# Light hops of a fused graph network: the edge-weight multiply moves from VectorE to GpSimd

## The reference

```python
def _L1_gnn_ref(ebds, edge_val, edge_row, edge_col, num_layers):
    def spmm(x):
        msgs = edge_val[:, None] * x[edge_col]
        return jax.ops.segment_sum(msgs, edge_row, num_segments=n)
    acc = ebds
    cur = ebds
    for _ in range(num_layers):
        cur = spmm(cur)
        acc = acc + cur
    return acc
...
h = jnp.maximum(_layernorm(x, axis=-1), 0.0)
x = x + _L1_gnn_ref(h, edge_weight, src, dst, 3)
```

## Time and profile before

| | |
|---|---|
| three runs | 6606.59, 6608.01, 6619.2 us |
| median | 6608.01 us |
| profiled execution | 6613.96 us, its span 6612.3 us |
| busy share of the span | DVE 64%, POOL 57%, PE 52%, ACT 44% |
| the phase touched | POOL's first gather at 2852.66 us, DVE's last chain of the third hop at 4061.5 us |
| length of the phase between its barriers | about 1,230 of 6,612 us |

### The profile page before, as it was taken

One profiled execution on the slowest core, in us unless ns is written; L12 is line 12 of the kernel. 1 busy time (PEld: TensorE's weight loads), 2 busy tenths in 40 slices (PEclk: granted clock), 3 DMA queues, 4 the chain that ended last, 5 costly groups with the idle time before them and its releaser, 6 DMA issues. The chain is left out here.

```text
span 6612.3 us, 76481 instructions
## 1 busy us (share of the span) xinstructions
PE 3439.3 (52%) x17336; PEld 2399.6 (36%) x17522; DVE 4231.7 (64%) x15945; ACT 2904.3 (44%) x7008; POOL 3787.8 (57%) x3751
## 2 busy tenths in 40 slices
PE   1527776501620000047777775888879994444443
PEld 0414555401620000024444443566546663433222
DVE  7369996361571646679999997777646664544332
ACT  1936775200300001146776764777647663322110
POOL 1655563676666734565353544666477635776777
PEclk9769997755865555568998987999989996656666
DMA  2225665408612264433344443555434435755333
GB/s 65 79 74 178 201 199 174 138 12 145 198 39 47 37 163 152 140 110 108 98 114 102 107 108 117 183 188 190 138 101 137 134 115 195 225 178 173 115 120 103
DMA packets 509434, 859.79 MB, mean 130 GB/s; under 512 B 109352, under 2 KB 169108, under 8 KB 507885
## 3 DMA queue, kind: packets, MB, share of 16 engines
q1 hardware_dynamic: 393227, 662.54, 31.4%
q0 software_dynamic: 115808, 192.94, 12.9%
HBM read 412.62 MB, written 454.37 MB: 131 GB/s over the span
## 5 line engine op out<-in xcount | busy, mean ns | idle before, releaser
L2936 POOL DMA_INDIRECT gcn_ring<-GT,gcn_index x588 | 586.2, 997 | 199.4 <-issue 171.0
L1578 POOL DMA_INDIRECT light_ring<-C,light_s_u x392 | 393.7, 1004 | 313.7 <-DVE light_acc L1621 206.3
L3037 DVE SCALAR_TENSOR_TENSOR gcn_acc<-gcn_acc,cont,gcn_ring 128x128 f32<-128x128 f32 x588 | 203.8, 347 | 565.7 <-DMA gcn_ring<-GT,gcn_index 564.5
L3119 PE MATMUL gcn_psA<-ident,gcn_h 128*128 128x128 f32 x588 | 153.6, 412 | 611.8 <-DVE gcn_h L3040 611.3
L3086 ACT ACTIVATE gcn_hT<-gcn_psA 128x512 f32<-128x512 f32 x147 | 87.9, 598 | 705.6 <-PE gcn_psA L3119 705.4
L3119 PEld LDWEIGHTS gcn_psA<-ident,gcn_h 128*128 128x128 f32 x588 | 99.3, 206 | 649.2 <-DVE gcn_h L3040 649.2
L1421 ACT ACTIVATE tail_h<-tail_x,tail_nmr,tail_std 128x128 f32<-128x128 f32 x784 | 320.6, 483 | 10.0 <-DVE tail_nmr L1352 10.0
L2190 POOL DMA_INDIRECT out<-source_x,source_own_u x196 | 194.3, 991 | 210.5 <-DVE source_x L2276 162.4
L1777 PE MATMUL so_ps<-ordered,shift 128*128 128x1 f32 x2 | 0.6, 363 | 560.2 <-DVE so_diag L1760 560.2
L476 POOL DMA_INDIRECT gat_rows<-T,src_u x196 | 186.2, 950 | 184.2 <-POOLq L1108 75.1
L476 POOL DMA_INDIRECT got_s<-TAB,src_u x196 | 197.6, 1008 | 163.9 <-DMA got_s<-TAB,src_u 66.7
(11 more groups left out here) (589 smaller groups left out, 13493.9 us busy)
## 6 DMA issues: line engine op xcount, KB each, us to landing
T<-front_t SPq DMA_DIRECT2D x196, 272.0 KB, 2.1
C<-light_acc SPq DMA_DIRECT2D x147, 256.0 KB
source_c<-C SPq DMA_DIRECT2D x147, 256.0 KB
GT<-source_r SPq DMA_DIRECT2D x147, 256.0 KB, 2.1
gcn_own<-GT SPq DMA_DIRECT2D x147, 256.0 KB
RC<-gcn_own SPq DMA_DIRECT2D x147, 256.0 KB
gat_rows_r<-RG SPq DMA_DIRECT2D x104, 264.0 KB
RG<-gat_rows SPq DMA_DIRECT2D x2, 12936.0 KB
```

Source lines behind the costliest of these rows:

```text
L1578: nc.gpsimd.indirect_dma_start(out=ring[:, n % RING, j, :], out_offset=None, in_=tables[h], in_offset=bass.IndirectOffsetOnAxis(ap=index[: ...
L2936: nc.gpsimd.indirect_dma_start(out=ring[:, n % RING, j, :], out_offset=None, in_=net.GT[i], in_offset=bass.IndirectOffsetOnAxis(ap=index[: ...
L3037: nc.vector.scalar_tensor_tensor(out=acc[:, n % 2, j, :], in0=before, scalar=net.cont[:, c:c + 1], in1=ring[:, n % RING, j, :], op0=ALU.mu ...
L3119: ins = nc.tensor.transpose(psA[n % 2][:, j * P:(j + 1) * P], h[:, n % 2, j, :], net.ident[:, :])
```

## The change

The multiply by the edge weights leaves DVE's queue and goes to POOL's. POOL does it three groups behind its gathers (BEHIND = 3): after the four gathers of group g it waits for the rows of group g-3 and multiplies them in place; after the last gathers of a hop it multiplies the last three. DVE keeps the wait on `weighed` and the chain.

```diff
--- before.py
+++ after.py
@@ -1543,7 +1543,7 @@
 
 
     s_ = net.S
-    RING, AR = 8, 6
+    RING, AR, BEHIND = 8, 6, 3
     total = HOPS * NG
     sums_of = lambda n: range(0) if n % HOP_STEPS >= SUM_STEPS or n // HOP_STEPS >= HOPS else range(
         n // HOP_STEPS * NG + n % HOP_STEPS * NG // SUM_STEPS, n // HOP_STEPS * NG + (n % HOP_STEPS + 1) * NG // SUM_STEPS)
@@ -1567,6 +1567,11 @@
                 nc.gpsimd.tensor_copy(s_u[:, :], s_.s[:, :]).then_inc(copied, 1)
                 nc.gpsimd.tensor_copy(at[:, :], s_.first_end[:, :]).then_inc(copied, 1)
                 pool.wait_ge(copied, 3)
+
+                def weigh(n):
+                    g, got = n % NG, ring[:, n % RING, :, :]
+                    pool.wait_ge(arrived[n % RING], 16 * S * (n // RING + 1))
+                    nc.gpsimd.tensor_tensor(got, got, s_.ew[:, g * S:(g + 1) * S].unsqueeze(2).to_broadcast([P, S, D]), ALU.mult).then_inc(weighed, 1)
                 for h in range(HOPS):
                     index = s_u if h else r_u
                     for g in range(NG):
@@ -1578,6 +1583,10 @@
                             nc.gpsimd.indirect_dma_start(
                                 out=ring[:, n % RING, j, :], out_offset=None, in_=tables[h],
                                 in_offset=bass.IndirectOffsetOnAxis(ap=index[:, c:c + 1], axis=0)).then_inc(arrived[n % RING], 16)
+                        if g >= BEHIND:
+                            weigh(n - BEHIND)
+                    for n in range((h + 1) * NG - BEHIND, (h + 1) * NG):
+                        weigh(n)
                     for k in range(AR):
                         pool.wait_ge(stored[k], 16 * len(range(k, (h + 1) * NG, AR)))
                     nc.gpsimd.indirect_dma_start(out=fix[h][:, :], out_offset=None, in_=tables[h + 1],
@@ -1607,9 +1616,6 @@
 
                 def sums(n):
                     g = n % NG
-                    got = ring[:, n % RING, :, :]
-                    v.wait_ge(arrived[n % RING], 16 * S * (n // RING + 1))
-                    nc.vector.tensor_tensor(got, got, s_.ew[:, g * S:(g + 1) * S].unsqueeze(2).to_broadcast([P, S, D]), ALU.mult).then_inc(weighed, 1)
                     v.wait_ge(weighed, n + 1)
                     v.wait_ge(cleared, 1)
                     if n >= AR:
```

## The result

| | before | changed |
|---|---|---|
| median, us | 6612.18 (4 runs) | 6683.44 (4 runs, 6680.51 to 6689.92) |
| ratio to before | | 1.0109, 95% 1.0091 to 1.0126 |
| profiled execution, us | 6613.96 | 6680.51, span 6678.8 |

The changed kernel is slower by 71 us; the forecast was +66, from 6608 to 6674.

A forecast was written before the change was run, and what follows sets the result against it. DVE was taken to bound two-group steps, ACT's string one-group steps. Removal -66, unhidden holds +111, start +18 and other hop starts and ends +3 gave +66 on 6608: 6674 us, range for 8 in 10 6603 to 6728.

The forecast's parts named there:

- the removal: Taking the multiply off DVE saves 1.38 us in each of 48 two-group steps, nothing in one-group steps: -66 us.
- the start: At the beginning of a hop, more gathers and POOL's multiplies precede DVE's first chains, shifting the whole pipeline: +18 us.
- first chain, group 3: DVE's first chain comes 14.3 us later, and the multiply of group 3 ends 17.7 us later than its chain started.
- The holds: DVE instructions with two SBUF inputs stand still during POOL's two-input multiply; 111 us not hidden, made of 45 + 66.
- the mean over phases: Hold cost averaged over all positions in DVE's step: 0.88 us a hold, +0.8 us a period, +39 us in all.
- the walk: One three-group period followed in order: holds hit beta, late chain and x3; 25.25 us against 24.15, +54 us in all.
- The floor: ACT's string x0T, h, yn sets 6.51 us from late place to gamma, so no step is shorter than 11.28 us.
- The length of the hold: POOL's multiply blocks DVE from 0.62 us before its recorded start to 0.13 before its end: 1.58 us.
- Rival B: The hold is no longer than POOL's instruction, 0.43 us each on average: 6616 us, no change that can be told; chance 0.18.
- Rival C: DVE is first nearly every time and POOL waits, so no holds and a faster kernel: 6563 us; chance 0.12.
- Rival D: POOL, its multiply stretched by DVE, becomes the bound: 6629 us at least, near 6700 with the holds; chance 0.20 with them.
- the starts of hops two and three: POOL starts two steps before DVE needs the first group; counted as 1 us for each of these hops.

The follow-up runs named there:

- the idle multiply: Changed kernel, but POOL multiplies into a scratch buffer nobody reads and DVE sums unweighted rows without waiting for it; disturbed runs, ratios to before 0.9927 and 0.992.
- the write-only fill: Like the idle multiply, but POOL fills a 128x1152 scratch tile with zeros, reading nothing; disturbed runs, ratios to before 0.9825 and 0.9835.
- the timed multiply: Changed kernel, with POOL's one or two multiplies per step held until DVE's x3 add is done; undisturbed 6553.35 against 6593.04 us before, ratio 0.9936.

## Why the prediction was right

By its own steps, with what the runs gave; the kernel with no multiply stands between before and changed, so its phase splits the loss.

| step | predicted | measured |
|---|---|---|
| the removal | -66 | 1149.7 - 1208.9 = -59 (ratio 0.9907: -61) |
| two steps without multiplies | 22.77 | 22.93 |
| holds and start, against no multiply | 111 + 18 + 3 = 132 | 1283.3 - 1149.7 = 134 |
| the start, first g2T against before | +18 | 82.0 - 62.7 = +19.3 |
| first chain, group 3 | +14.3, +17.7 | +13.5, +15.8 |
| two steps changed | 25.25 | 25.45 |
| POOL's multiply | 1.09 | 1.05 |
| sum | +66 | +71 (phase +74) |

**The holds** were the deciding term, and the forecast had them right in kind (the idle multiply has them, the write-only fill and the timed multiply don't) and in place (beta, late chain, x3). The excess of chain, beta, x3 and gamma is 146 us, 0.99 a multiply, where the mean over phases gave 0.88. Of it, 134 less the start's 23.9 (first g2T 82.0 against 58.1) = 110 us isn't hidden; predicted 111. That this agrees to 1 us is luck: the 111 was made of a net 45 and a removal of 66, and behind the first g2T the runs give a net 74.4 - 19.3 = 55 and a removal of 55. The two misses, of 10 and 11 us, cancel in the 111; in the sum the net stayed 10 us too small. Between the walk (+54) and the mean (+39) I took +45; the walk, which followed actual positions, was the better of the two, and its 1.1 us for two steps is the measured difference of the means (24.80 - 23.66 = 1.14). Its three places are those of the middle of a hop only.

**The floor** is shown by the kernel with no multiply: gamma's idle time for yn is 72.7 us there, 28.2 before. The term, 66, was too large. Behind the first g2T the removal gave back 1146.2 - 1091.6 = 55 us, and another 4.6 came at the start (first g2T 58.1 against 62.7), where none was counted. The step that was off is "11.49, still above the floor": the floor of 6.51 us from late place to gamma was read from one row, but ACT's yn comes at 7.20 us or later in steps where DVE alone needs 6.7, so 18 of 43 two-group steps run into it, and give back 1.20 us in the mean instead of 1.38. What moves is the start of x0T, which waits for PE's psF (2.1 to 3.1 us behind the late place in the steps of 6.19 and 7.20 us); from x0T to gamma it is 4.07 us. Why psF comes at different times was not looked into.

**The length of the hold.** 0.62 + 1.09 - 0.13 = 1.58 was drawn from two rows, and it holds in many: of the 57 instructions in which a multiply starts, the one that was furthest on had started 0.61 us ahead of POOL; in the kernel whose product nobody uses, 72 of 74 were held, and the two that weren't had started 0.66 and 0.67 us ahead. Beta's first row in the period above starts 0.37 us before POOL's multiply and loses 1.3, and the x3 row starts 0.48 us after POOL's recorded start and loses only 0.44: 3173.25 + 0.44 = 3173.69, 0.13 us before POOL's end at 3173.82. So the end of the hold, 0.13 us before POOL's recorded end, came out again. Beta's own work began at 3158.24 + 1.31 = 3159.55, 0.12 before the end at 3159.67. The prediction's sentence on these rows says too much, though: with an add of 1.28 us its hold of 0.62 + 1.28 - 0.13 = 1.77 us is 0.5 us longer than the instruction and not 0.6, and if the one that issues first were the one that keeps going, the trace doesn't agree, since by the recorded starts DVE was first there (4112.54 against 4113.16), as in all 57. Whether POOL issues earlier than its record says is open. Rival B, a hold that is no longer than the instruction, had foretold half the loss; it falls with the 0.99 us a multiply. Rival C (DVE first, POOL waits) falls with beta's 1263 ns. Rival D falls with the 140.8 us for which POOL still waits for DVE; its multiply isn't stretched either, 1051 ns in the mean.

**Counted, but not met**: the tiny nmr instructions stood among those that are held, after the 1.77 us row. They can be: in the timed kernel their maximum is 1594 ns. In the changed kernel it is 203 ns, since POOL's multiplies never fell on them. And the starts of hops two and three cost nothing: 20.9 us from first gather to first chain, 20.6 before.

## What to carry to other kernels

Before arithmetic goes to an idle GpSimd, ask what VectorE does at that moment, not only how much room GpSimd has: here an instruction of 1.05 us with two SBUF inputs took 0.99 us from VectorE's two-input instructions beside it, more than the 0.66 us it relieved VectorE of. The same move with the same instructions gains once a semaphore puts it beside VectorE's PSUM and one-input stretch (ratio 0.9936 against 1.0111). And find the floor first, over many steps and not in one row: of 101 us removed from the busiest engine, only some 60 came back, the rest turned into a wait for the next engine.

## What the runs showed that was not expected

- A GpSimd fill of 128x1152 (1.08 us), as frequent as the multiply, leaves VectorE's two-input instructions at 348 and 681 ns, though it starts in the middle of one 94 times: this fill could stand anywhere.
- In the middle of a hop the three multiplies of a period come back to the same three places (beta 1.99 and 2.19, late chain 2.83 and 2.83 us in two periods in a row). POOL's gathers are released by the chain's end, so a hold delays its own successor too; that this is what locks the two queues is argued, not tried.
- In the timed kernel two steps took 24.6 us disturbed and 22.93 undisturbed; TensorE's mean clock over the phase was 0.87 and 0.90, with stretches at 0.50 behind a wait in the first. How much of the 1.7 us is the clock and how much the standstills stays open.
- On one occasion TensorE stood still 110 to 140 times a launch in each kernel traced, mostly for 2 to 25 us, and the kernel before took some 870 us longer. The order of the kernels by time was another one: the kernel with one group behind came out below before, the one with no multiply above it. In the light phase the latter had 26 and 32 standstills of over 5 us in its two runs, the six other runs 2 to 4. The cause isn't in these profiles; lengths of instructions could be compared there, times not.
